# Interleaving pairs of small matmuls on TensorE, together with a new written-out order of all engines

## The reference

```
x = x + gate * (attend(mod(LN(x)), keys/values) @ Wo + bo)      # seven times
x = x + gate * (act(mod(LN(x)) @ Wup + bup) @ Wdown + bdown)    # three times
attend: 16 heads of 8 features, softmax(q k^T / sqrt(8)) v
```

## Time and profile before

| | |
|---|---|
| median of 3 runs | 672.29 us (669.69 to 678.34) |
| profiled execution, its own time | 665.29 us |
| its span, first to last instruction | 663.5 us |
| mean granted TensorE clock | 0.863 of full |
| PE busy | 570.0 us (86%) |
| DVE busy | 490.9 us (74%) |
| ACT busy | 386.3 us (58%) |
| POOL busy | 306.4 us (46%) |

### The profile page before, as it was taken

One profiled execution on the slowest core, in us unless ns is written; L12 is line 12 of the kernel. 1 busy time (PEld: TensorE's weight loads), 2 busy tenths in 40 slices (PEclk: granted clock), 3 DMA queues, 4 the chain that ended last, 5 costly groups with the idle time before them and its releaser, 6 DMA issues.

```text
span 663.5 us, 14489 instructions
## 1 busy us (share of the span) xinstructions
PE 570.0 (86%) x5152; PEld 378.9 (57%) x5152; DVE 490.9 (74%) x1291; ACT 386.3 (58%) x669; POOL 306.4 (46%) x584
## 2 busy tenths in 40 slices
PE   3888989899999999999998889786999987867477
PEld 3645556566756565657665556554655664634246
DVE  2577767853859687745377727999999999999953
ACT  2546878799696887886757766452233531611133
POOL 6884535435845444364562446641341446111133
PEclk9858999999999999998989979777575795765779
DMA  9560344302333533020335043140020002000000
GB/s 319 143 159 3 88 106 112 73 2 54 76 67 69 105 77 78 2 65 2 66 72 123 2 129 68 28 101 0 2 65 2 2 10 64 9 1 2 1 2 16
DMA packets 15062, 39.23 MB, mean 59 GB/s; under 512 B 2641, under 2 KB 6801, under 8 KB 14737
## 3 DMA queue, kind: packets, MB, share of 16 engines
q0 software_dynamic: 8960, 29.37, 20.1%
q1 hardware_dynamic: 5312, 8.46, 3.8%
q10 hardware_dynamic: 720, 0.49, 0.3%
HBM read 7.96 MB, written 0.52 MB: 13 GB/s over the span
## 4 chain that ended last, share of the span: by engine, by line
DVE 38%; PE 37%; ACT 8%; DMA 6%; issue 6%; POOL 4%; ACTq 0%; POOLq 0%
PE psum L1590 10%; DVE left L1419 8%; DVE left L1429 7%; DVE top L1426 6%; DVE top L1416 6%; DVE maxima L1406 5%; PE psum L1566 5%; PE psum L1536 5%; ACT softmax_T L1298 4%; DMA qk_stack<-centred 3%; PE psum L1625 3%; PE psum L1636 3%; DMA qk_stack<-qk_parts 2%; DVE maxima L1402 2%; PE psum L1617 2%
## 5 line engine op out<-in xcount | busy, mean ns | idle before, releaser
L1298 ACT ACTIVATE softmax_T<-psum 128x1024 f32<-128x1024 f32 (+1 forms) x224 | 210.9, 962 | 111.7 <-PE psum L1577 73.3
L1406 DVE TENSOR_REDUCE maxima<-psum 128x4 f32<-128x1024 f32 x160 | 190.1, 1216 | 52.4 <-PE psum L1536 51.6
L1566 PE MATMUL psum<-qk_stack 32*128 32x256 f32 (+1 forms) x896 | 114.9, 346 | 28.1 <-DMA qk_stack<-centred 9.6
L1590 PE MATMUL psum<-softmax_T,values 128*32 128x256 f32 (+1 forms) x1792 | 129.9, 408 | 4.8 <-ACT softmax_T L1298 3.5
L1566 PEld LDWEIGHTS psum<-qk_stack 32*128 32x128 f32 x896 | 72.3, 202 | 71.0 <-issue 31.0
L1227 POOL TENSOR_SCALAR unpicked<-left 128x512 bf16<-128x512 f32 x64 | 39.5, 616 | 136.0 <-DVE left L1429 135.3
L1536 PE MATMUL psum<-qk_stack 32*128 32x256 f32 (+1 forms) x768 | 89.6, 335 | 9.2 <-ACT softmax_T L1298 2.4
L1536 PEld LDWEIGHTS psum<-qk_stack 32*128 32x128 f32 x768 | 58.9, 200 | 37.5 <-issue 16.5
L1590 PEld LDWEIGHTS psum<-softmax_T,values 128*32 128x32 f32 x1792 | 56.7, 118 | 40.3 <-issue 12.0
L1187 POOL TENSOR_TENSOR qk_parts<-qk_parts 128x256 fp32r<-128x256 f32 x56 | 40.9, 730 | 77.0 <-ACT qk_parts L1281 76.6
L1158 POOL DMA_DIRECT2D qk_stack<-qk_parts x112 | 63.7, 580 | 7.0 <-POOL qk_parts L1187 6.3
(11 more groups left out here) (99 smaller groups left out, 870.3 us busy)
## 6 DMA issues: line engine op xcount, KB each, us to landing
qk_stack<-qk_parts POOLq DMA_DIRECT2D x112, 256.0 KB, 5.1
weights<-in_w SPq DMA_DIRECT2D x1, 1408.0 KB, 13.5
row_biases<-in_rows SPq DMA_DIRECT2D x1, 1088.0 KB, 10.8
weights<-in_w SPq DMA_DIRECT2D x2, 512.0 KB, 5.9
weights<-in_w SPq DMA_DIRECT2D x1, 832.0 KB, 9.0
qk_stack<-centred SPq DMA_DIRECT2D x48, 8.0 KB
weights<-in_w SPq DMA_DIRECT2D x1, 768.0 KB, 4.3
weights<-in_w SPq DMA_DIRECT2D x1, 576.0 KB, 3.7
```

The costliest lines, as they stand in the source:

```text
L1298: nc.scalar.activation(pT[:, slot, u % 2, :, 0:cols].rearrange("p (i t) n -> p i t n", t=NT), two_banks(step).rearrange("p i (t n) -> p i ...
L1406: nc.vector.tensor_reduce(rows[:, u // 4, u // 2 % 2, g:g + 2, :], ps.rearrange("p i (t k) -> p i t k", t=NT), AX_X, ALU.max).then_inc(fin, 1)
L1566: ins = nc.tensor.matmul(ps[:, i, t, 0:P if window else N], QKS[b][32 * g:32 * g + 32, s, 1, P * t:P * t + P], QKS[b][32 * g:32 * g + 32, ...
L1590: ins = nc.tensor.matmul(misc[32 * g:32 * g + 32, queries], V[:, b, t, first:first + 32], pT[:, slot, g // 2, 2 * (g % 2) + t, 0:P if wind ...
```

## The change

1. **Interleaved pairs.** `plan` may now take two PE steps together: when it picks a full `scores`, a non-topk `weights` or a `topk` step, it looks for a second such step on disjoint row groups whose inputs are in (planned) no more than 0.15 us later and for which banks are free. The code waits for the banks and inputs of both, then issues first half of one, first half of the other, second half of one, second half of the other. To let a step pair with its neighbour, a `scores` or `weights` step with odd u no longer depends on the one before it in its layer (`scores` of window layers, and `topk` and `weights` of layer 6, keep that dependence).
2. **Constant rows.** POOL waits for `k_rows_s` only ahead of its first `stack` step.
3. **Norm.** The negated mean (L1168) goes; the centring step subtracts the mean as it stands in `mean_var`.
4. **Planning.** A row of maxima is planned to arrive 1.5 us after its issue plus up to 3.0 us for stack transfers queued ahead, before a flat 2.2 us. Statistics are planned from 6.7 us (before 5.9), the context from 10.2 us (before 9.0). `LEAD`, `BIAS` and `EXTRA` (some 400 numbers) are new throughout, so every engine's list is a new one.

```diff
+ROWS_WAY, ROWS_BEHIND = 1.5, 3.0
+WOVEN, WOVEN_BESIDE, WOVEN_FIRST, WOVEN_SECOND, WOVEN_SLOWER, TOGETHER = 0.44, 0.1, 0.42, 0.43, 1.67, 0.15
+def weaves(step):
+    kind, b, l, u = step
+    if kind == "topk":
+        return True
+    return kind == "scores" and ATTN[l]["kind"] == "full" or kind == "weights" and ATTN[l]["kind"] != "topk"
...
-                    pe = task("pe", ("scores", b, l, u), stack[planes_of_scores(l, u)[-1]], t and ("pe", ("scores", b, l, u - 1)))
+                    pe = task("pe", ("scores", b, l, u), *[stack[s] for s in planes_of_scores(l, u)],
+                              ("pe", ("scores", b, l, u - 1)) if u and (u % 2 == 0 or lay["kind"] == "window") else None)
...
-                t = task("pe", ("weights", b, l, u), maxed[u // 2], prev and ("pe", ("weights", b, l, u - 1)),
+                t = task("pe", ("weights", b, l, u), maxed[u // 2], ("pe", ("weights", b, l, u - 1)) if u and (u % 2 == 0 or topk) else None,
...
+        if eng == "pe" and weaves(step):
+            others = [(rank(n), c[0], n) for n in ready["pe"] if (c := choose(n)) is not None]
+            fit = [o for o in others if weaves(o[2][1]) and not groups(o[2]) & groups(t) and o[1] <= s + TOGETHER]
+            if fit:
+                r, at, other = max(fit, key=lambda o: o[0])
+                if any(r + BESIDE < o[0] for o in others if o not in fit and o[1] <= s + 0.3):
+                    other = None
...
-            land = end + TO_QUEUE + 0.3
+            land = end + ROWS_WAY + min(max(0.0, queue - end - 0.64), ROWS_BEHIND)
...
-LEAD = [[29.6, 27.3, 159.8, 27.1, 27.2, 25.2, 30.7, 27.0, 78.1, 420.1],
-        [18.3, 18.3, 18.3, 19.7, 18.7, -13.4, -10.7, -63.6, 338.4, -332.4],
-        [9.3, 9.1, 50.8, 7.5, 8.8, 525.5, 13.5, -500.4, -1.8, 224.2],
-        [1.3, 1.4, 437.2, -0.3, 0.9, -1.2, 4.4, 87.9, 52.7, -9.6]]
+LEAD = [[26.3, 27.0, 26.2, 27.2, 26.8, 26.3, 27.9, 204.4, 84.3, 1115.0],
+        [18.0, 18.0, 15.8, 18.3, 19.1, 18.2, 19.7, 18.1, 82.3, -179.8],
+        [8.9, 8.9, 291.3, 9.2, 8.7, 198.0, -7.0, 0.2, -60.1, -428.6],
+        [0.9, 0.8, 632.9, 1.7, 0.5, 1.1, 2.6, 557.6, -71.3, -20.2]]
...
-            pool.wait_ge(k_rows_s, 16 * SLOTS["qk"])
+            first_stack = next(i for i, s in enumerate(ORDERS["pool"]) if s[0] == "stack")
...
+                    if step == ORDERS["pool"][first_stack]:
+                        pool.wait_ge(k_rows_s, 16 * SLOTS["qk"])
...
-                    nc.gpsimd.tensor_scalar(nmean[:, b, c, :], mv[:, b, c, :, 0], -1.0, 0.0, ALU.mult, ALU.add)
...
-                        ins = nc.gpsimd.tensor_scalar(dst[:, b, t, :], src[:, b, t, :], nmean[:, b, c, t:t + 1],
-                                                      rstd[:, b, c, t:t + 1], ALU.add, ALU.mult)
+                        ins = nc.gpsimd.tensor_scalar(dst[:, b, t, :], src[:, b, t, :], mv[:, b, c, t, 0:1],
+                                                      rstd[:, b, c, t:t + 1], ALU.subtract, ALU.mult)
...
             for step in ORDERS["pe"]:
+                if step in WOVEN_WITH.values():
+                    continue
...
+                if weaves(step):
+                    inputs_in(step)
+                    if step in WOVEN_WITH:
+                        other = WOVEN_WITH[step]
+                        banks_free(pe, other)
+                        inputs_in(other)
+                        half(step, 0)
+                        half(other, 0)
+                        half(step, 1).then_inc(fin, 1)
+                        half(other, 1).then_inc(done[other[0], "pe"], 1)
+                    else:
+                        half(step, 0)
+                        half(step, 1).then_inc(fin, 1)
```

More of the change, by code:

```diff
@@ L205 @@
[L205 to L209, removed]
@@ L221 @@
[L221 to L225, removed]
@@ L566 @@
[L566 to L571 removed]
+    ("act", "context"): 63.7, ("act", "heads_out"): 1.2, ("act", "k_parts"): 21.6, ("act", "maxima"): 3.2,
@@ new lines @@
+    ("act", "mix"): -0.4, ("act", "normed"): 67.2, ("act", "qk"): -0.2, ("act", "up"): 305.2,
+    ("act", "values"): 7.2, ("act", "weights"): 1.1, ("dve", "divide"): 28.3, ("dve", "down"): 99.0,
+    ("dve", "gates"): 86.5, ("dve", "mods"): -65.7, ("dve", "pbias"): -52.3, ("dve", "residual"): 133.2,
+    ("dve", "scores"): 122.7, ("dve", "stats"): -70.1, ("dve", "topk"): -28.9, ("dve", "topk_rest"): -146.7,
+    ("dve", "up_gate"): 48.6, ("pe", "context"): -40.9, ("pe", "divide"): -0.4, ("pe", "down"): -1.8,
@@ new lines @@
+    ("pe", "gates"): -1.7, ("pe", "heads_out"): 0.1, ("pe", "mods"): -1.0, ("pe", "normed"): -0.2,
+    ("pe", "pbias"): -7.0, ("pe", "residual"): -0.1, ("pe", "topk"): -29.2, ("pe", "up"): 0.6,
+    ("pe", "up_gate"): 27.7, ("pe", "values"): -6.5, ("pool", "gated"): 5.5, ("pool", "k_parts"): 3.0,
+    ("pool", "pre"): -1.8, ("pool", "qk"): 464.9, ("pool", "stack"): 3.2, ("pool", "topk"): -215.8,
+    ("pool", "z"): 2.1, ("sp", "load"): -69.6, ("sp", "maxima"): -36.7, ("sp", "store"): 104.2,
+}
@@ L753, in transfer @@
         return 0.195 * (WGROUPS[step[2] + 1] - WGROUPS[step[2]])
-    lands = {"stack": TO_QUEUE + STACK_TIME + LANDS, "maxima": TO_QUEUE}
+    lands = {"stack": TO_QUEUE + STACK_TIME + LANDS, "maxima": ROWS_WAY}
     users = {t: [] for t in order}
@@ L782, in plan @@
     lists = {e: [] for e in engines}
-    clock, spare = Clock(), {}
+    clock, spare, woven = Clock(), {}, {}
     table, last, queue = "exp", 0, 16.0
@@ L843, in choose, with hold, landing @@
         return s, taken
+    def hold(t, taken):
+        for ring, which in taken:
+            slots[ring] = [o for o in slots[ring] if o not in which]
+            slot[ring, t[1]] = [k for _, k, _ in which]
+            had[ring, t[1]] = sorted({before for _, _, before in which if before is not None})
+    def landing(t, land, end):
+        for r, taker in gives(t):
+            slots[r] += [(land + HOP, k, taker) for k in slot[r, taker]]
+            slots[r].sort()
+        for n in users[t]:
+            waiting[n] -= 1
+            ready_at[n] = max(ready_at[n], land + (HOP if n[0] != t[0] or land > end else 0.02))
+            if not waiting[n]:
+                ready[n[0]].append(n)
     left = len(order)
@@ L871, in plan @@
         d, lag = busy(t), 0.0
+        since = max([free["pe"], IDENTITY_THERE] + [when for _, which in taken for when, _, _ in which])
+        hold(t, taken)
+        other = None
[5 more added lines that the diff above has]
+                if any(r + BESIDE < o[0] for o in others if o not in fit and o[1] <= s + 0.3):
+                    other = None
+        if eng == "pe" and taken and s - since >= IDLE:
+            clock.until(since)
+            spare[step] = int(min(0.85 * (s - since), 0.3 + 0.6 * (s - since)) * (1.0 if clock.rate == 1 else 1 / 1.8) / SPARE_D)
+            if spare[step]:
+                clock.run(since, spare[step] * SPARE_D, spare[step] * SPARE_CELLS, 1.8)
+        if other is not None:
+            s = max(s, at)
+            d = WOVEN - (WOVEN_BESIDE if beside(t, s) else 0.0)
+            last = groups(other)
+            end = clock.run(s, d, cells(step) + cells(other[1]), WOVEN_SLOWER)
+            ready["pe"].remove(other)
+            hold(other, choose(other)[1])
+            free["pe"] = end
+            woven[step] = other[1]
+            for n, land in ((t, WOVEN_FIRST), (other, WOVEN_SECOND)):
+                land = s + (end - s) / d * land
+                done[n] = (s, land)
+                lists["pe"].append(n[1])
+                landing(n, land, end)
+            left -= 2
+            continue
         if beside(t, s):
@@ L880, in plan @@
                 table = fn
-        if eng == "pe" and taken:
-            since = max([free["pe"], IDENTITY_THERE] + [when for _, which in taken for when, _, _ in which])
-            if s - since >= IDLE:
-                clock.until(since)
-                spare[step] = int(min(0.85 * (s - since), 0.3 + 0.6 * (s - since)) * (1.0 if clock.rate == 1 else 1 / 1.8) / SPARE_D)
-                if spare[step]:
-                    clock.run(since, spare[step] * SPARE_D, spare[step] * SPARE_CELLS, 1.8)
         end = clock.run(s, d, cells(step), SLOWER.get(kind, 1.8)) if eng == "pe" else s + d
@@ L891, in plan @@
         lists[eng].append(step)
-        for ring, which in taken:
-            slots[ring] = [o for o in slots[ring] if o not in which]
-            slot[ring, step] = [k for _, k, _ in which]
-            had[ring, step] = sorted({before for _, _, before in which if before is not None})
         land = end + lag
@@ L906, in plan @@
         elif eng == "sp" and kind == "maxima":
-            land = end + TO_QUEUE + 0.3
-        for r, taker in gives(t):
-            slots[r] += [(land + HOP, k, taker) for k in slot[r, taker]]
-            slots[r].sort()
-        for n in users[t]:
-            waiting[n] -= 1
-            ready_at[n] = max(ready_at[n], land + (HOP if n[0] != eng or land > end else 0.02))
-            if not waiting[n]:
```

(36 more changed lines are left out.)

467 lines of the change are left out of this document (228 added, 239 removed), and 333 rows, old and new, of the table EXTRA.

## The result

Over 20 runs each, the changed kernel takes 678.15 us in the median (672.66 to 691.86) and the kernel before 669.78 (663.28 to 678.34); the ratio is 1.014, 95% interval 1.0109 to 1.0171. Some executions of every kernel show a lower granted clock and a longer time; medians in us are of all executions, ratios compare only those without it. The forecast was 648 us, with a range that ended at 672. The profiled execution took 675.88 us, its span is 674.1 (before 663.5).

What follows compares the result with a forecast made beforehand. PE was taken to bound the first stage, DVE the second. From 665.3 us, 20 for pairs, 3.3 for the start and 0.5 for negated means gave 641.5, or 648 us in the runs' terms; range 628 to 672.

Steps and rivals of the forecast that it cites:

- (b): Rival: PE's pair saving is taken by other bounds, as neighbours already overlap and few new pairs form; 664 us, chance 0.26.
- (c): Rival: joint waits for two inputs and two bank pairs outweigh the pairs, making the kernel slower; 692 us, chance 0.10.
- Subtracting mean directly uses the same instruction over 128 elements: POOL's norm: the centring step's subtract costs what the add did, 0 and a few ns either way.
- I pass on 0.75: First stage: of 26 us less PE work from pairs, 20 us arrive in the time, from 7 to 35 us.
- the turning point: PE's pairs: above a mean joint wait of 26 / 120 = 0.22 us a pair, the saving is gone.
- 45% of the pairs: First stage: existing mixed-line pairs with nothing to gain, 33 of 73; the other 49 of 89 pairs give 11 to 12 us.
- Half of the singles would pair: First stage: 119 single steps form 30 new pairs, saving 12 to 13 us of PE's work.
- The start: POOL's first norm 2.5 us earlier, first stack 0.8 us from negated means; together 3.3 us, between 1 and 3.5.
- The 0.8 us for the negated means: Start: four negated means of 0.19 us stand serially ahead of the first stack; removing them saves 0.8 us.
- The orders: Every engine's new list: fewer row waits and added joint waits cancel, 0 us, from -7 to +10.
- (a): Rival: batches reach layer 6 sooner and top-k fills DVE's idle time, 15 us on top; 633 us, chance 0.14.
- PE's relief: PE's work ahead of the DVE stage falls by 26 us, between 13 and 39, through pairs.

Runs made afterwards that it cites:

- f3: Changed kernel with the old norm and its 69 pairs issued one after the other, each with its own waits: 662.14 us, 0.9908 of the kernel before.
- e1: Changed kernel with the old norm (negated mean, add) put back: 671.11 us, 0.9956 of the kernel before.
- g2: Changed kernel, new norm included, with its 69 pairs issued one after the other with their own waits: 673.45 us, 1.0058 of the kernel before.
- e3: Kernel before with only the wait for the constant rows moved to the first stack: 665.98 us, 0.9950.
- e2: Kernel before with only the new norm (mean subtracted, no negated mean): 677.38 us, 1.0153.
- g1: f3 with the wait for the constant rows back in its old place, so the new orders alone: 664.40 us, 0.9891 of the kernel before.
- e4: Kernel before, orders untouched, with 103 neighbour pairs issued half by half after joint waits: 683.10 us, 1.0227.
- g3: Kernel before with the mean copied into the packed tile and subtracted in the centring step: single run, 682.84 us.
- f1: Kernel before with e4's 103 pairs and joint waits, but one step issued after the other: 685.86 us, 1.0190.

## Why the prediction was wrong

| part | forecast, us | measured, us of about 670 |
|---|---|---|
| pairs | -20 | +3 to +6 (f3 to e1, g2 to the change) |
| moved wait | -2.5 | -3.4 (e3), not seen on top of the new orders |
| new norm | -1.3 with its part of the start | +10 (e2) to +12 (e1 to the change) |
| new orders | 0 (-7 to +10) | -7 (g1) |

Of the 30 us between 648 and 678, the pairs are the larger part (23 to 26 us) and the norm the second (11 to 13); the orders came out 7 us better. The measured time lies between those of the rivals (b), 664, and (c), 692.

- **"Subtracting mean directly uses the same instruction over 128 elements: 0, and a few ns either way."** This step failed, and it decides the sign: without the new norm the change stands at 0.9956. The trace of before had no POOL tensor_scalar that subtracts, so the cost had to be bounded by rows that are unlike it; I took the price of the add as if the operation had none of its own. The profile gave no warning: of POOL's two-tensor steps over 128x256, the subtract (L1187) takes 730 ns and the add (L1219) 728. The centring measured +350 ns, 96 times.
- **"I pass on 0.75" of 26 us of pairs.** The arithmetic of PE's work held where pairs were made: e4 takes some 14 us off PE's busy time (564.8 against g3's 578.9) where existing pairs and those at the lower clock were to give 11 to 12 and 3, and a pair costs 0.44 us. The step that failed is that any of this time would arrive. In the order of before it came with joint waits that are larger: rival (c)'s mechanism, at its price per pair. e4's waits rise by 24 us over the 99 pairs that start from 20 to 420 us, 0.24 us each; the turning point named was 0.22. In the new orders the loss is 3 to 6 us, and its mechanism is not shown apart. The rival had a chance of 0.10, since row waits summed to only 7.1 us; the waits that grew were those for banks held by DVE's maxima and ACT's exponentials, which I had put into one sentence and not priced.
- **"Neighbours already overlap without being told" (b).** Right, and stronger than I used it: f1 shows that the written-out halves add nothing. Counting 45% of the pairs as already together and the rest as gain missed why the rest were not together. The trace of before has the answer in its semaphores: of the some 40 mixed pairs that start more than 0.1 us apart, 31 have the last signal that the second step waits for no more than 0.06 us ahead of its start. Nearly all are pairs with a late partner, and the weave can only wait for it.
- **Half of the singles would pair, 30 pairs.** The new plan has 69 pairs in all, fewer than the 89 neighbours that the order before had in the first stage alone. Its own written order has 129 neighbours that e4's rule would join, so `plan` left many apart. Whether the four banks of a pair or the limit of 0.15 us keep the number down, no run shows.
- **The Trainium skill's rule** ("TensorE: Matmul & The Clock Gate", Part 3, "The mechanism": matmuls start in program order) doesn't agree with f1, where in 96 places the second step starts with the first against the order of the program; the earlier trace rows had shown it.
- **The start.** "2.5 us earlier" for POOL's first norm was right (6.95), and e3's 3.4 us (0.9 to 5.8) fits it. The 0.8 us for the negated means was never tried alone. In the changed kernel four norms that are 0.5 us longer use 2 of the 2.5 us up before the first stack.
- **The orders.** The value 0 was not right: 7 us less, at the very end of the range, on the side of rival (a). The mechanism fits (a) as well, DVE's solid stage being fuller from 400 us on in f3 and g1; that this is what shortens them is argued, not tried by itself.
- **Busy time of PE** was to fall by 25 to 45 us; it rose by 10, and the 66 more matmuls on the identity account for that (36.9 us on them, against 27.4 before). Parts measured apart give 0.9908 (f3) x 1.0048 (pairs, e1 over f3) x 1.0153 (norm, e2) = 1.011, the lower end of the change's interval, 1.0109 to 1.0171; what is left, 0.3%, is no more than the intervals of the parts.
- **Small slips**, on which nothing rests: PE's digits up to 400 us are 8 and 9, not all 9, and from 430 us they go down to 6; DVE's lie between 2 and 9. The lower end of PE's relief adds up to 14 us, not 13, and the chance of faster to 0.65, not 0.64.

## What to carry to other kernels

Price an instruction by a row with the same operation on the same engine; where there is none, measure it by itself before it goes into a chain of forty norms. Before weaving two steps by hand, look in the trace whether the engine already runs them together when both are ready: if it does, look for what those still apart wait for, since a joint wait brings that wait forward to the first of them and to all that is queued behind it. A fall in busy time is no gain until the count of instructions done in the same stretch has been looked at.

## What was not expected of the hardware

GpSimd's tensor_scalar on 128x128 float32 takes 447 ns as add then multiply, and 797 ns as subtract then multiply, with the scalar packed or strided alike. TensorE started matmuls of a later step ahead of an earlier step's second half where the two lay on different row groups with nothing to wait for: some 33 times in the kernel before, 96 times in f1, with 0.44 us for the eight.
